# Turned heads and turned maxima in other PSUM banks, and a fourth bank for queries' scores

## What is computed

```python
q, k = split(x @ W_attn + b_attn); v = x            # 16 heads each
y  = causal_attention(q, k, v)
e  = v[:, :, 1:] - y[:, :, :-1]                     # values of the second attention
k2 = x[:, :-1] @ W_k2 + b_k2
y2 = causal_attention(q[:, :, 1:], k2, e)           # a zero row put ahead
x  = layernorm(x + proj(y) + proj(y2))
x  = layernorm(x + ffn(x))                          # experts of routed tokens, first 512 tokens
```

## Time and profile before

| | |
|---|---|
| median of three runs | 2544.13 us (2540.0 to 2548.04) |
| the profiled execution | 2552.98 us, span 2551.2 us |
| busy share of the span | TensorE 95%, VectorE 83%, ScalarE 69%, GpSimd 59% |
| instructions | TensorE 19670 matmuls, VectorE 9397, ScalarE 3388, GpSimd 2342 |
| mean granted TensorE clock | 0.982 of full speed |
| DMA engines busy | some 53% of 16 engines' span |

### The profile page before, as it was taken

One profiled execution on the slowest core, in us unless ns is written; L12 is line 12 of the kernel. 1 busy time (PEld: TensorE's weight loads), 2 busy tenths in 40 slices (PEclk: granted clock), 3 DMA queues, 4 the chain that ended last, 5 costly groups with the idle time before them and its releaser, 6 DMA issues.

```text
span 2551.2 us, 65289 instructions
## 1 busy us (share of the span) xinstructions
PE 2431.7 (95%) x19670; PEld 1277.8 (50%) x19670; DVE 2128.1 (83%) x9397; ACT 1758.5 (69%) x3388; POOL 1507.4 (59%) x2342
## 2 busy tenths in 40 slices
PE   2999999999999999999999999999999999999997
PEld 1555555555555555555455555454555555455454
DVE  2888888888988888889888888888888888888655
ACT  0377777677777777777777777776777777677652
POOL 2366665666666656666666566666656666566432
PEclk8699999999999999999999999999999999999998
DMA  5555555565555555655555566554555655455211
GB/s 96 92 106 91 97 95 102 102 119 106 108 98 100 99 99 105 119 106 107 92 94 107 97 113 118 107 98 89 99 98 107 119 106 106 88 96 101 51 55 54
DMA packets 187783, 251.24 MB, mean 98 GB/s; under 512 B 26768, under 2 KB 103192, under 8 KB 187416
## 3 DMA queue, kind: packets, MB, share of 16 engines
q1 hardware_dynamic: 187440, 247.07, 52.1%
HBM read 74.60 MB, written 16.78 MB: 36 GB/s over the span
## 4 chain that ended last, share of the span: by engine, by line
PE 71%; DVE 13%; issue 7%; DMA 3%; POOL 2%; SPq 2%; ACT 1%; DVEq 0%; ACTq 0%; POOLq 0%
PE score_t L643 22%; PE out_t L604 20%; PE misc L710 9%; DVE junk L845 8%; PE score L654 7%; PE misc L746 5%; PE turn L686 4%; DMA resid<-L_attn_x 2%; PE score L794 2%; SPq L351 1%; DVE max_cols L845 1%; PE misc L733 1%; DVE stats L276 1%; PE score L810 1%; DVE resid L896 1%
## 5 line engine op out<-in xcount | busy, mean ns | idle before, releaser
L845 DVE CUSTOM_DVE_ANT_0 junk<-score,mask_rows 128x384 bf16<-128x384 f32 (+3 forms) x3584 | 1685.9, 515 | 310.8 <-PE score L654 307.6
L513 ACT ACTIVATE prob<-score_t 128x512 f32<-128x512 f32 x2560 | 1399.8, 599 | 576.3 <-PE score_t L643 574.1
L424 POOL TENSOR_SCALAR_AFFINE_SELECT prob<-prob 128x512 f32<-128x512 f32 (+1 forms) x1280 | 711.2, 559 | 832.4 <-ACT prob L513 829.4
L643 PE MATMUL score_t<-stack_q,stack_k 50*128 50x128 f32 (+5 forms) x4096 | 1074.1, 367 | 36.5 <-ACT prob L513 17.5
L654 PE MATMUL score<-stack_k,stack_q 48*128 48x512 f32 (+3 forms) x4096 | 1063.5, 355 | 14.1 <-DMA stack_q<-part_l 12.0
L643 PEld LDWEIGHTS score_t<-stack_q,stack_k 50*128 50x128 f32 (+1 forms) x4096 | 609.0, 185 | 652.8 <-ACT prob L513 539.5
L604 PE MATMUL out_t<-prob,value 128*17 128x512 f32 (+3 forms) x8192 | 719.9, 438 | 12.9 <-POOL prob L424 12.9
L654 PEld LDWEIGHTS score<-stack_k,stack_q 48*128 48x128 f32 x4096 | 616.0, 188 | 26.8 <-DVE max_cols L845 12.6
L845 DVE DVE_READ_ACCUMULATOR2_ANT max_cols<- 128x1 f32 x4096 | 338.5, 83 | 0.0
L604 PEld LDWEIGHTS out_t<-prob,value 128*17 128x17 f32 x8192 | 166.7, 96 | 334.2 <-issue 203.8
L446 POOL TENSOR_TENSOR part_l<-part_f,part_h 128x512 fp32r<-128x512 f32 x192 | 245.9, 1281 | 16.3
(11 more groups left out here) (98 smaller groups left out, 1714.7 us busy)
## 6 DMA issues: line engine op xcount, KB each, us to landing
stack_k<-part_h SPq DMA_DIRECT2D x512, 128.0 KB, 4.2
stack_k<-part_l SPq DMA_DIRECT2D x256, 128.0 KB, 4.5
stack_q<-part_h SPq DMA_DIRECT2D x256, 128.0 KB, 4.2
x_full<-x_turned SPq DMA_DIRECT2D x32, 512.0 KB, 10.8
x_in<-L_attn_x SPq DMA_DIRECT2D x32, 512.0 KB, 14.2
stack_q<-part_l SPq DMA_DIRECT2D x128, 128.0 KB, 5.1
resid<-L_attn_x SPq DMA_DIRECT2D x32, 512.0 KB, 7.8
layer_out<-resid SPq DMA_DIRECT2D x31, 512.0 KB, 5.3
```

Source lines behind the costliest of these rows:

```text
L424: e.affine_select(out=view, in_=view, compare_op=ALU.is_ge, fill=0.0, base=-unit_parts(unit)[1], pattern=[[0, runs], [0, cut], [1, P]], ch ...
L513: e.activation(prob[pair % RING][:, slot % 2 * 512:slot % 2 * 512 + 512], score_t[time % KEY_DEPTH][:, :], ACT.Exp, scale=1.0 / np.sqrt(HE ...
L643: done = e.matmul(score_t[now % KEY_DEPTH][:, col:col + n], keys[rows, pair, kb * P:(kb + 1) * P], stack_q[b % 2][rows, pair, kb * P:token ...
L845: e.tensor_tensor_reduce(junk[count % JUNK][:, 0:n], score[number % MAX_DEPTH][:, col:col + n], mask, 1.0, -3e38, ALU.add, ALU.max, max_co ...
```

## The change

Three places change their bank, and the bank that comes free is given to the queries' scores:

- The turned heads are written to `out_t`, from which they came, in place of `turn`. So the next unit's first weighting, which starts to fill `out_t` again, now waits until VectorE has normalised (`s_normal`) and not only until ScalarE has copied the heads (`s_heads`). VectorE's normalisation is issued in slot 5 instead of slot 6.
- The turned maxima are written to `misc`. They wait there for the piece before, and the next writers of `misc` wait for `neg_l`: the piece of place 7 and the first output projection of place 3. The waits that guarded `turn` are gone.
- `MAX_DEPTH`, the number of `score` banks, goes from 3 to 4.

```diff
-RING, KEY_DEPTH, MAX_DEPTH, JUNK = 6, 2, 3, 2
+RING, KEY_DEPTH, MAX_DEPTH, JUNK = 6, 2, 4, 2
...
-        turn = ps("turn", 512)
...
-                        e.activation(neg_h[:, :], turn[0:64, 0:P], ACT.Copy, scale=-1.0).then_inc(s_negh, 1)
+                        e.activation(neg_h[:, :], misc[0:64, 0:P], ACT.Copy, scale=-1.0).then_inc(s_negh, 1)
...
@@ TensorE, slot 7 @@
                     if unit:
-                        e.wait_ge(s_heads, unit)
+                        e.wait_ge(s_normal, unit)
                     weigh(unit, 0, 0, tokens, start=True)
...
                 if slot == 5 and 0 <= unit - 1 < end:
                     e.wait_ge(s_heads, unit)
-                    if unit >= 2:
-                        e.wait_ge(s_normal, unit - 1)
-                    if place == 7 and ahead + 1 < batches:
-                        e.wait_ge(s_negl, 2 * (ahead + 1) + 1)
-                    if place == 3:
-                        e.wait_ge(s_negl, 2 * ahead + 2)
                     for t in range(blocks):
-                        done = e.transpose(turn[:, t * P:(t + 1) * P], heads_t[:, t * P:(t + 1) * P], ident[:, :])
+                        done = e.transpose(out_t[:, t * P:(t + 1) * P], heads_t[:, t * P:(t + 1) * P], ident[:, :])
...
@@ TensorE, pieces @@
+                            if place == 7 and ahead + 1 >= 0:
+                                e.wait_ge(s_negl, 2 * ahead + 3)
...
@@ TensorE, turned maxima, slot 1 of places 7 and 3 @@
-                        if unit >= 2:
-                            e.wait_ge(s_normal, unit - 1)
-                        e.transpose(turn[0:64, 0:P], max_cols[b % 2][:, a, :, :, :].rearrange("p s h q -> p (s h q)"),
+                        e.wait_ge(s_full, min(N_PIECES * (b + 1) + (4 if a else 0), N_PIECES * batches))
+                        if ahead >= 1:
+                            if a:
+                                e.wait_ge(s_yt, halves * ahead)
+                            else:
+                                e.wait_ge(s_attended, 2 * ahead)
+                        e.transpose(misc[0:64, 0:P], max_cols[b % 2][:, a, :, :, :].rearrange("p s h q -> p (s h q)"),
...
@@ TensorE, output projection, place 3, slot 3 @@
+                                        if ahead < batches:
+                                            e.wait_ge(s_negl, 2 * ahead + 2)
...
@@ VectorE @@
-                        e.scalar_tensor_tensor(out=neg_l[:, :], in0=turn[0:64, 0:P], scalar=-1.0, in1=neg_h[:, :].bitcast(F32),
+                        e.scalar_tensor_tensor(out=neg_l[:, :], in0=misc[0:64, 0:P], scalar=-1.0, in1=neg_h[:, :].bitcast(F32),
...
-                if slot == 6 and 0 <= unit - 1 < end:
+                if slot == 5 and 0 <= unit - 1 < end:
                     b, a, g = unit_parts(unit - 1)
-                    heads = turn[:, :].rearrange("p (t h w) -> p t h w", t=blocks, h=GROUP)
+                    heads = out_t[:, :].rearrange("p (t h w) -> p t h w", t=blocks, h=GROUP)
```

## The result

| | before | after |
|---|---|---|
| median of four runs each | 2546.09 us | 2633.23 us (2629.26 to 2643.7) |
| ratio, with its 95% interval | 1 | 1.0351 [1.0314, 1.0388] |
| the profiled execution | 2552.98 us, span 2551.2 | span 2642.0 us |
| mean granted TensorE clock | 0.982 | 0.981 |

The account below looks back on a forecast made before the run. TensorE's own order was taken to bound the kernel; new waits and restarts less gains made +3.49 us a batch over 31 batches, less some 2 us: 106 us on the median 2544.13, so 2650 us, range 2600 to 2680.

Parts of the forecast that it names:

- The new wait on the first weighting: TensorE's first weighting of the next unit waits for VectorE's normalisation, up to +1.09 us, in place 4.
- The output projection: At place 3, slot 3, the projection writes misc and so waits for neg_l: +0.39 us.
- The fourth bank: Scores need the maxima of slot n-4, not n-3, removing waits in places 0, 1, 5 and 7: -0.78 us.
- the normalisation a slot sooner: On VectorE, same instructions filling its 0.56 us wait before slot 6's scores; nothing extra on TensorE beyond what was counted.
- 0.78 + 0.08 - 0.28: Per batch: fourth bank's gain, place 5 weighting waits covered by the new wait, and TensorE's net restart cost.
- GpSimd's masks are not touched: TensorE's waits for GpSimd's masks stay as they were, except some 0.08 us in place 5's weighting.
- The sum: All terms together: +3.49 us a batch, applied to 31 of 32 batches, less some 2 us: 106 us.
- Rival 1: Stalls do not add up: held in place 3, TensorE waits no more in places 4, 5, 7; 2588 us, chance 0.11.
- Rival 2: Faster: normalisation done before TensorE reaches the first weighting, fourth bank's 1.02 us a batch remains; 2512 us, chance 0.03.
- Rival 4: No change: losses fall in waits on ScalarE and GpSimd that exist anyway; 2544 us, chance 0.03.
- rival 3: The clock falls: more short stops cost TensorE its granted clock, adding some 110 us; 2760 us, chance 0.05.
- one of my own signs of being wrong: A granted TensorE clock below 1.00 between 115 and 1743 us.

Follow-up runs that it names:

- e2: Kernel before, heads and maxima keeping their own bank, with only normalisation in slot 5 and the first weighting waiting for it: 2636.65 us.
- e4: Kernel before with only the maxima turned in misc and the waits that go with it: 2553.93 us.
- e1: Changed kernel with three banks of queries' scores in place of four: 2639.94 us.
- e3: Kernel before with only the normalisation issued in slot 5 instead of slot 6: 2602.06 us.
- e13: Kernel before with the normalisation in slot 5 and GpSimd's addition of the bias to the residual moved behind the masks: 2535.97 us.
- e9: Kernel before with GpSimd's addition of the bias to the residual in slot 9 of place 2 instead of slot 5, behind the masks: 2524.25 us.
- e10: Changed kernel with GpSimd's addition of the bias to the residual in slot 9 of place 2 instead of slot 5: 2593.02 us.
- e6: Changed kernel with the normalisation ahead of slot 5's maxima and neg_l ahead of slot 2's: 2534.84 us.
- e12: Changed kernel with normalisation ahead of slot 5's maxima, neg_l ahead of slot 2's, and the bias addition in slot 9 of place 2: 2512.29 us.
- e8: e12 with place 4's statistics in slots 1, 2, 6 and 7 instead of 1 to 4, and the aggregation in slot 7: 2539.68 us.

## Why the prediction was right

The direction, the mechanism and the places were right; two sizes were wrong in opposite ways, and one wait was missing.

- **The new wait on the first weighting.** Predicted +0.62, +1.09, +0.82, +0.81 and +0.16 us in places 3 to 7 and 0.06 in each of the others; measured +0.53, +1.04, +0.79, +0.78, +0.12 and nothing (medians over the batches; in places 0 to 2 the spacing from slot 4's scores is 3.04, 2.84 and 2.83 us, as it was). The release took 0.10 us from the end of the product (0.06 in place 3), not the 0.15 read at the maxima's read-out. e2 shows the loss with this wait and the sooner normalisation alone, and no bank shared.
- **The output projection.** Predicted +0.39, measured +0.36 us (slot 2's to slot 4's scores: 3.14 to 3.50). e4 has it alone, at 8.6 us.
- **The fourth bank: the wrong step.** I put -0.78 us down to it. e1 and e2 show the same short units in places 0, 1 and 7 with three banks, so it gave nothing in the batches and 4 to 5 us at the start. The paragraph on the normalisation a slot sooner ("It costs the same instructions and now fills the 0.56 us") failed with it. In places 0, 1 and 5 the move lets slot 8's maxima, for which the next unit's scores wait, come earlier (e3); alone it holds back slot 6's maxima, 0.6 us in each of places 3 and 4 (e13). The score waits were not for lack of a bank but for work standing ahead of the maxima.
- **What came back.** With the mask's wait out (e9, e10) a batch costs 2.41 us (without the one slow unit of e9's trace), of which the new waits are 3.62 (the sum of the first two points), so 1.21 came back; my sum had 0.78 + 0.08 - 0.28 = 0.58.
- **The wait for the mask: left out.** I had written that waits on "GpSimd's masks are not touched". The instructions are not, but the wait grows by 3.09 - 2.41 = 0.68 us a batch, nearly all in place 3. Places 0 and 1 are 0.4 us shorter, and the residual's transfer does not follow: measured from the start of place 3 it lands 1.7 us ahead in the kernel before (1.6 in e9) and 1.3 ahead in the changed one (1.0 in e10), in the median. How much of that is the shorter units and how much the transfer itself is not shown; with the same short units it landed 0.3 us ahead in e3 and e13, and 1.7 in e6 and e12.
- **The sum.** Against 3.49 us a batch, 3.09 were measured: waits 0.45 less (4.07 predicted), 0.63 more back, 0.68 more at the mask. That is 12 us of the 17 by which 2650 was too high; the start (3.5 us sooner) is most of the rest. That it was no more is partly luck: the gain that I had missed and the wait that I had left out cancel.
- **The rivals.** Rival 1 fell: places 4 and 5 hold their full waits. Rival 2 fell with it. Rival 4 too. Of rival 3 a little was true, and with it one of my own signs of being wrong came: the clock over the long stretch was 0.99 where it was 1.00:

```profile
115.00:1743.00 1628.00, 1533.90 (x12935) 801.37 (x12935) 1381.93 (x6169) 1144.41 (x2215) 984.57 (x1531) 0.99 0.55 98
```

  In the unit of 643.7 us it was 0.81 after 2.20 us of standing still at the mask. From unit 16 to 245 the changed kernel's trace has five such spells at the 1.2 GHz level, 30.6 us in all, each in place 3 behind a stop of 1.7 to 3.5 us at the mask; the kernel before has two, 6.8 us, in the same place behind 1.8 and 1.9 us. At half the clock the 23.8 us more are at most some 12 us of work, an estimate, and part of what stands above as the mask's wait. In e10, with the first weightings' waits of up to 1.1 us but without the mask's, it is 1.00 over the same stretch. So the new waits by themselves did not lower it. "TensorE: Matmul & The Clock Gate" (Trainium skill, A second HAM failure mode) tells of a kernel in which short idle times between groups of matmuls made the clock swing between its levels. e10's trace does not show that, with stops of 0.5 to 1.1 us four times a batch; e8's does, with one of 1.15 us.

## What to carry to other kernels

Where a result is put back into the bank it came from, the bank's next writer waits for the reader of the result; price that wait from the reader's place in its own engine's queue, place by place, and look first whether the reader can go ahead of the work in front of it. A wait for lack of a buffer and a wait for work queued ahead of the buffer's release look alike in the list; taking the buffer away again tells them apart. And an instruction that waits at the head of a queue passes its wait on to all behind it, however small it is itself: a residual's addition ahead of masks cost 23 us here, and a logarithm of 0.21 us ahead of exponentials 27 us, some 8 of them by the clock.

## What the runs showed of the hardware that I had not expected

A TensorE matmul started 0.06 to 0.11 us after the end of the VectorE product that it waited for, in all of the places shown. Between units 16 and 245 the granted clock fell to the 1.2 GHz level for some us at a time, in these traces always behind a stop of TensorE, but not only behind long ones. In the changed kernel it was 0.81 over the 17.6 us that contain a stop of 2.20 us. In e8 a stop of 1.15 us, the same in every batch, was followed by such a spell in nine batches of 29; this is the one of the unit shown above:

```profile
429.30:432.60 3.30, 3.30 (x28) 1.03 (x20) 1.53 (x7) 1.72 (x4) 2.88 (x10) 0.50 0.00 0
```

Once, in e9's slow unit, it followed a stop of 0.84 us. Stops of 0.5 to 1.1 us, four a batch, left it at 1.00 in e10:

```profile
115.00:1743.00 1628.00, 1541.65 (x13193) 810.85 (x13191) 1411.04 (x6300) 1168.78 (x2261) 1007.85 (x1563) 1.00 0.56 101
```

What sets the batches with a spell apart from those without, no run shows.
